# Self attention with its keys first, and cross attention's small steps at other places of its pipeline

## The chip, the cores and the metric

The kernel runs on 1 core of one Trainium2 chip, in one launch. The metric is the device time of one execution in microseconds (us); the time before is 2896.58 us, the median of 3 runs (2896.07 to 2899.03).

## The reference

Two Flamingo layers on x (16 x 56 x 256), each a gated attention block and a gated feed-forward block. What the change touches is the second layer's attention, which reads x and a context of 16 x 1500 x 256:

```python
ln_out = _ln(hidden_states, ln_w, ln_b)
q = _ln(_fp8_linear_pertensor(ln_out, wq, wq_scale, q_in_scale).reshape(b, s, g, hpg, d), qln_w, qln_b)
k = _ln(_fp8_linear_pertensor(ln_out, wk, wk_scale, k_in_scale).reshape(b, s, g, d), kln_w, kln_b)
v = _fp8_linear_pertensor(ln_out, wv, wv_scale, v_in_scale).reshape(b, s, g, d)
core = _gqa(q, k, v).reshape(b, s, nh * d)                 # self attention, 16 heads on 8 key groups
qx = _ln(_fp8_linear_pertensor(ln_out, wqx, ...), qxln_w, qxln_b)
kx, vx = jnp.split(jnp.einsum('bsi,oi->bso', cond, w_kv_x), 2, axis=-1)
xout = _gqa(qx, _ln(kx, kxln_w, kxln_b), vx)               # cross attention on 1500 context rows
cat = jnp.concatenate([core, xout], axis=-1)
catq = _div_clamp_fp8(cat, proj_smooth)                    # divide, clamp, round to fp8
```

`_fp8_linear_pertensor` scales its input per channel, clamps it and rounds it to fp8 before the product; `_gqa` is a softmax attention with two query heads for each key group.

## The kernel before

The program is a row of stages with a barrier of all engines between them. The change touches `self_attention` (L727) and `cross_attention` (L1217), and in `context_statistics` (L121) one index, by which the order of the scaled weight chunks is told.

**Self attention** goes over 8 pairs of batches (112 rows, a "turn"). A turn has 12 chunks of 4 heads (512 columns): 4 of the queries q, 4 of the cross attention's queries qx, 2 of the keys, 2 of the values. PE projects chunk t + 2 in slot t (L1016, high and low part of the weights). Each of the 10 normed chunks then runs through the engines: square on ACT (L900), sum of squares on DVE (L1127), root on ACT (L906), reciprocal and product on DVE (L1134, L1136), transposes on PE (L1027), scale and bias on ACT (L933). Tables of slots (L778 to L780) say where the rest lies: `SCORES` (PE L1037, L1040), `MAXIMA` (DVE L1142, L1146), `EXPS` (ACT L940), `SUMS` (DVE L1151, L1154 and POOL L865), `TURNED` (PE L1049), `VALUES` (ACT L946, PE L1060) and `OUTPUT` (DVE L1158 to L724, POOL L869, L874), each for four groups of heads of the turn before. `SCALED` and `QUANTISED` place the fp8 rounding of the inputs for the next two turns (ACT L953, DVE L1119 to L724, POOL L857, L861), one for each of q, qx, k and v: its parts go ACT, DVE, POOL, and the next one's scaling waits for them. Slots 12 and up of a table are slots of the turn after. Two turns make one pass of the loop; the body before lets the odd turn end with two roundings of inputs and two outputs. After the last turn, slots without chunks finish its attention.

**Cross attention** goes over 16 batches of 2 units (4 key groups, 448 query columns), 6 steps a unit, and each step treats 2 of the 12 context tiles of 125 rows. In step i, PE computes scores (L1468, 12 matmuls) and, 10 steps behind, the values (L1505, 12 matmuls); DVE takes the scores out of PSUM (L1556, s_sx), subtracts the maximum 8 steps behind (L1574), forms the low part of exp (L1580, s_p_lo) and the running maximum (L1593, s_mxh; in step 5 also L1598, s_mx); ACT does exp (L1422) and the high part (L1427); POOL adds the exps up (L1355, L1358, in step 1 also the last sum, L1361) and, in steps 1, 3 and 5 of a batch's second unit, splits the context (L1366, s_cn_lo). Around them lie the small steps, once a unit: step 0 transposes the maxima (PE L1514) and reduces them (DVE L1585); steps 1 and 2 fold the next unit's queries (PE L1445), which ACT and DVE split (L1383, L1541); step 2 spreads the maxima (L1475) and sums the exps of the unit two back (L1528), whose reciprocal (DVE L1569, step 3) ACT and PE spread (L1404, L1480, L1417, steps 3 and 4); step 5 multiplies by the value weights (PE L1489). One PSUM bank, `misc`, holds transposes, folds, sums, spread reciprocals and value products in turn. Step 0 of the next unit then multiplies products and reciprocals (DVE L1561, s_ca), rounds them (DVE L1602 to L1606; POOL L1370, L1374) and SP stores them (L1317). SP's queue is in order: it also loads the context in both layouts (L1299, L1300, L1305) and the queries (L1311), each load behind a wait for its buffer.

## Time and profile before

| | |
|---|---|
| median of 3 runs | 2896.58 us (2896.07 to 2899.03) |
| the profiled execution | 2896.9 us, its span 2895.1 us, mean granted clock 0.940 |
| PE, DVE, ACT, POOL busy | 88%, 74%, 38%, 32% of the span |
| self attention | 1033 to 1400 us of the span |
| cross attention | 1400 to 2660 us |

Busy shares are of the whole span; what a part costs is read from the stretch of its stage. The profile's own execution is 0.3 us above the median. The granted clock is given as a share of 2.4 GHz, so 0.5 is 1.2 GHz.

### The profile page before, as it was taken

The numbers are of one execution on the slowest core, as the hardware profiler recorded it, in microseconds if no ns is written. First come the engines' busy times: TensorE is split into PE (matmuls) and PEld (weight loads), VectorE is DVE, ScalarE is ACT, GpSimd is POOL, SyncE is SP. The second block draws the span as 40 slices with busy tenths as digits, with TensorE's granted clock in tenths as the row PEclk, the third lists the DMA queues.
The fourth block names the chain that finished last, engine by engine and source line by source line (L and its number), as shares of the span: only waits on it lengthen the run. The fifth ranks groups of instructions, "written<-read, shape, count | busy, mean of one in ns | idle before, by whom it ended". The sixth has DMA issues, their size and how long they took to land. (4 is left out here: it accounts for less than half of the span.)

```text
span 2895.1 us, 39559 instructions
## 1 busy us (share of the span) xinstructions
PE 2545.1 (88%) x13434; PEld 2221.3 (77%) x13434; DVE 2156.1 (74%) x3892; ACT 1100.6 (38%) x1787; POOL 928.2 (32%) x584
## 2 busy tenths in 40 slices
PE   7999999939999957777699999999999999986797
PEld 5777777738999945666588888888888888875797
DVE  8777777773333367777488889999999999993377
ACT  1000000014444445556144444545444444444332
POOL 6560000000000012443255555555555555553000
PEclk9999999969999958888799999999999999998899
DMA  6444333120111030101322122222222222213311
GB/s 240 182 172 158 137 143 135 55 73 30 59 44 44 0 115 26 39 39 39 118 73 70 62 73 73 73 73 71 70 66 68 69 69 65 65 38 86 103 50 40
DMA packets 116412, 231.89 MB, mean 80 GB/s; under 512 B 22176, under 2 KB 94704, under 8 KB 112240
## 3 DMA queue, kind: packets, MB, share of 16 engines
q1 hardware_dynamic: 112880, 218.35, 22.2%
q0 software_dynamic: 3456, 12.58, 1.1%
q8 instruction: 40, 0.66, 0.1%
q14 instruction: 36, 0.29, 0.0%
HBM read 158.95 MB, written 71.96 MB: 80 GB/s over the span
## 5 line engine op out<-in xcount | busy, mean ns | idle before, releaser
L1358 POOL TENSOR_TENSOR s_acc<-s_acc,s_sx 125x896 f32<-125x896 f32 x128 | 356.4, 2784 | 249.0 <-ACT s_sx L1422 248.9
L290 DVE BATCH_NORM_STATS2 s_st<-ps 125x6 f32<-125x128 f32 x1536 | 316.2, 286 | 114.2 <-PE ps L246 112.4
L1422 ACT ACTIVATE s_sx<-s_sx 125x896 f32<-125x896 f32 x192 | 184.0, 959 | 461.4 <-DVE s_sx L1574 461.3
L1505 PE MATMUL ps<-s_p_hi,s_cn_hi 125*128 125x448 f32 x768 | 297.7, 388 | 7.3 <-DVE s_p_lo L1580 6.9
L1468 PE MATMUL ps<-s_qc_hi,s_ct_hi 128*125 128x448 f32 x768 | 294.5, 383 | 1.3 <-issue 1.3
L1556 DVE TENSOR_TENSOR s_sx<-ps,keep_krs 125x896 f32<-125x896 f32 x192 | 208.7, 1087 | 106.8 <-PE ps L1468 103.2
L1468 PE MATMUL ps<-s_qc_lo,s_ct_hi 128*125 128x448 f32 x768 | 286.0, 372 | 0.0
L1468 PE MATMUL ps<-s_qc_hi,s_ct_lo 128*125 128x448 f32 x768 | 285.4, 372 | 0.0
L1505 PE MATMUL ps<-s_p_lo,s_cn_hi 125*128 125x448 f32 x768 | 283.1, 369 | 0.0
L1505 PE MATMUL ps<-s_p_hi,s_cn_lo 125*128 125x448 f32 x768 | 282.8, 368 | 0.0
L246 PE MATMUL ps<-s_wk_hi,s_hi 128*125 128x512 f32 x768 | 246.5, 402 | 40.3 <-DVE s_st L290 21.8
L1580 DVE TENSOR_TENSOR s_p_lo<-s_sx,s_p_hi 125x896 fp32r<-125x896 f32 x192 | 264.3, 1377 | 4.9 <-ACT s_p_hi L1427 4.9
L845 POOL MEMSET s_mask<- 112x112 f32 x1 | 0.2, 185 | 794.9 <-POOLq L432 794.9
L246 PE MATMUL ps<-s_wk_hi,s_lo 128*125 128x512 f32 x768 | 243.3, 398 | 0.0
L246 PE MATMUL ps<-s_wk_lo,s_hi 128*125 128x512 f32 x768 | 243.3, 398 | 0.0
L666 DVE TENSOR_TENSOR s_g_lo<-s_g,s_g_hi 128x898 fp32r<-128x898 f32 x64 | 70.1, 1096 | 214.4 <-ACT s_g_hi L495 214.4
L229 ACT ACTIVATE s_hi<-s_raw 128x3000 fp32r<-128x3000 f32 x16 | 43.4, 2714 | 470.4 <-PE ps L246 466.3
L1574 DVE TENSOR_TENSOR s_sx<-s_sx,ps 125x896 f32<-125x896 f32 x192 | 206.4, 1075 | 1.1
L246 PEld LDWEIGHTS ps<-s_wk_hi,s_hi 128*125 128x125 f32 x768 | 143.3, 188 | 82.1 <-DVE s_st L290 28.4
L1593 DVE TENSOR_TENSOR s_mxh<-s_mxh,s_sx 125x896 f32<-125x896 f32 x128 | 197.7, 1545 | 0.1
L1427 ACT ACTIVATE s_p_hi<-s_sx 125x896 fp32r<-125x896 f32 x192 | 183.1, 954 | 11.3 <-DVE s_p_lo L1580 4.3
L246 PEld LDWEIGHTS ps<-s_wk_lo,s_hi 128*125 128x125 f32 x768 | 144.9, 189 | 37.3
(303 smaller groups left out, 6054.9 us busy)
## 6 DMA issues: line engine op xcount, KB each, us to landing
s_raw<-in_ctxt SPq DMA_DIRECT2D x16, 1500.0 KB, 7.3
ct_hi<-s_hi SPq DMA_DIRECT2D x16, 1500.0 KB, 10.4
ct_lo<-s_lo SPq DMA_DIRECT2D x16, 1500.0 KB, 13.6
s_ct_hi<-ct_hi SPq DMA_DIRECT2D x48, 500.0 KB, 3.8
s_ct_lo<-ct_lo SPq DMA_DIRECT2D x48, 500.0 KB, 4.5
s_cn_raw<-in_ctx SPq DMA_DIRECT2D x48, 500.0 KB
s_w<-in_w SPq DMA_DIRECT2D x16, 1024.0 KB, 5.3
qx<-s_qxs SPq DMA_DIRECT2D x16, 448.0 KB, 2.8
```

Of the source, the lines that this page charges most:

```text
L246: mm = pe.matmul(kx[0:TT, t % NB, h, :], a[:, k, TT * t:TT * t + TT], w[:, k, 512 * h:512 * h + 512], start=(n == 0), stop=(n == 5))
L290: ins = dve.bn_stats(st[:, G * t + g, :], kx[0:TT, t % NB, g // 4, DH * (g % 4):DH * (g % 4) + DH])
L666: dve.tensor_tensor(g_lo[r][:, :], g32[r][:, :], g_hi[r][:, :].bitcast(F32), ALU.subtract).then_inc(s["g_lo_ready"], 1)
L1358: pool.tensor_tensor(a, a, p[:, PR * w.pt:PR * w.pt + PR, :], ALU.add).then_inc(s["acc_ready"], 1)
L1422: act.activation(p, p, ACT.Exp).then_inc(s["exp_ready"], 1)
L1427: act.activation(p_hi[w.pr][:, :, :], p, ACT.Copy).then_inc(s["hi_ready"], 1)
L1468: mm = pe.matmul(sc[st % 2][:, j, :], a[:, k, at:at + TT], x[w.h][:, k, :], start=(c == 0), stop=(c == 5))
L1505: mm = pe.matmul(pv[:, k, :], x[:, t, k * P:k * P + P], y[w.vr][:, j, :], start=(t == 0 and c == 0), stop=(t == NT - 1 and c == 2))
L1556: dve.tensor_tensor(by_group(sx[w.h][:, tiles, :]), by_group(sc[st % 2]), krs_b[:, tiles, HG * w.h:HG * w.h + HG].unsqueeze(3).to_broadcas ...
L1574: dve.tensor_tensor(p, p, mb.unsqueeze(1).to_broadcast([TT, PR, QH]), ALU.subtract).then_inc(s["sub_ready"], 1)
L1580: dve.tensor_tensor(p_lo[w.lr][:, :, :], p, p_hi[w.lr][:, :, :].bitcast(F32), ALU.subtract).then_inc(s["lo_ready"], 1)
L1593: dve.tensor_tensor(mxh[:, :, :], a, sx[w.h][:, tiles, :], ALU.max).then_inc(s["mxh_ready"], 1)
```

## The change

Self attention: the chunks come in the order keys, q, qx, values. The scores of a turn then lie in slots 7 to 10 of the same turn and their maxima in 8 to 11; exps, sums, turned probabilities and values in slots 0 to 7 of the next, the outputs in 5, 6, 7 and 12 of it. The inputs' roundings lie in slots 4 (v) of an even turn, and 4 (k), 10 (q) and 11 (qx) of an odd one; three of them, not four, come ahead of the first turn. The side work on the key weights moves from slots 8 and 9 to 4 and 5 of the first turn.

Cross attention: the sums' matmuls move on PE from the end of step 2 to step 3, behind its scores and ahead of its values; DVE's second split of the folded queries comes first in step 3; the product s_ca moves to step 5 of the unit before, ahead of the running maximum; the rounding on DVE and POOL moves to step 3; SP's stores go one place back, behind the load of the next batch's queries and first context chunk, the second one into the next batch.

```diff
+PART = [0] * NQ + [1] * NQ + [2] * NK + [3] * NK
+TURN_OF = [2, 0, 1, 3]
+ORDER = [c for part in TURN_OF for c in range(CHUNKS) if PART[c] == part]
+KIND = [TURN_OF.index(PART[c]) for c in ORDER]
...
-        SCORES, MAXIMA, EXPS = (0, 1, 2, 3), (1, 2, 3, 4), (5, 5, 5, 5)
-        SUMS, TURNED, VALUES, OUTPUT = (6, 7, 7, 8), (8, 9, 10, 11), (9, 10, 11, CHUNKS), (10, 11, CHUNKS, CHUNKS + 5)
-        SCALED, QUANTISED = ({}, {7: 0, 9: 1, 10: 2, 11: 3}), ({0: 3}, {8: 0, 10: 1, 11: 2})
+        SCORES, MAXIMA, EXPS = (7, 8, 9, 10), (8, 9, 10, 11), (CHUNKS,) * 4
+        SUMS, TURNED = [tuple(CHUNKS + t for t in ts) for ts in ((1, 2, 2, 3), (3, 4, 5, 6))]
+        VALUES, OUTPUT = [tuple(CHUNKS + t for t in ts) for ts in ((4, 5, 6, 7), (5, 6, 7, CHUNKS))]
+        SCALED, QUANTISED = ({3: 3}, {3: 0, 9: 1, 10: 2}), ({4: 3}, {4: 0, 10: 1, 11: 2})
...
-                for kind in range(4):
+                for kind in range(3):
                     round_input(0, kind)
...
                 def scores(q, a):
-                    if a == 0:
-                        pe.wait_ge(s["tr_read"], NORMED * q + NORMED)
+                    pe.wait_ge(s["tr_read"], NORMED * q + NK + a + 1)
...
@@ cross attention, SP @@
                     for c in range(NCH):
                         load_cn(b, c)
+                    if not first(b) and not (static(b) and b == 1):
+                        store(b - 2, 1)
                     if more:
                         load_q(b + 1)
+                        load_ct(b + 1, 0)
                     if not first(b):
                         store(b - 1, 0)
                     if more:
-                        load_ct(b + 1, 0)
                         load_ct(b + 1, 1)
-                    if not first(b):
-                        store(b - 1, 1)
-                    if more:
                         load_ct(b + 1, 2)
@@ POOL @@
-                    if w.i == 0 and w.three_back:
+                    if w.i == 3 and w.three_back:
@@ PE @@
+                    if w.i == 3 and w.two_back:
+                        pe.wait_ge(s["acc_ready"], NPR * (w.u - 1))
...
+                        for j in range(HG):
+                            mm = pe.matmul(sums[:, j:j + 1], acc[w.h][:, 0, PAIR * j:PAIR * j + PAIR], keep.ones[0:TT, 0:1], start=True, stop=True)
+                        mm.then_inc(s["sum_ready"], 1)
@@ DVE @@
+                    if w.i == 3 and w.next and w.new:
+                        qc_split(w.u + 1, 1 - w.h, 1)
                     if w.new:
                         dve.wait_ge(s["sc_ready"], w.n + 1)
...
+                    if w.i == NPR - 1 and w.two_back:
+                        dve.wait_ge(s["rb_read"], w.u - 1)
+                        dve.wait_ge(s["v_ready"], w.u - 1)
+                        dve.tensor_tensor(ca[:, :], misc[:, 0:QH], rsc[:, :], ALU.mult).then_inc(s["v_read"], 1)
...
+                    if w.i == 3 and w.three_back:
+                        dve.wait_ge(s["v_read"], w.u - 2)
+                        if not (static(b) and w.u < 4):
+                            dve.wait_ge(s["cat_ready"], w.u - 3)
+                        dve.tensor_scalar(cb[:, :], ca[:, :], FP8_MAX, -FP8_MAX, ALU.min, ALU.max).then_inc(s["cb_ready"], 1)
...
```

How the instructions stand on DVE at the end of an odd turn of self attention, before: the last input's rounding of slot 11, then slot 0 with the third output and another input (s_ca to s_cc is an output, s_xb to s_xc an input).

```order
L1158 TENSOR_TENSOR s_ca<-ps,keep_rsmooth 128x448 [waits s4_pv_ready]
L1163 TENSOR_SCALAR s_cb<-s_ca 128x448 [waits s4_cat_ready,s4_pv_read]
L723 TENSOR_SCALAR s_ce<-s_cb 128x448 [waits s4_dve_steps]
L724 TENSOR_SCALAR s_cc<-s_ce 128x448 [waits s4_dve_steps]
L1119 TENSOR_SCALAR s_xb<-s_xs 128x448 [waits s4_xs_ready,s4_xq_ready]
L723 TENSOR_SCALAR s_xe<-s_xb 128x448 [waits s4_dve_steps]
L724 TENSOR_SCALAR s_xc<-s_xe 128x448 [waits s4_dve_steps]
L1134 RECIPROCAL s_hrs<-s_hstd 112x4 [waits s4_tr_ready,s4_hstd_ready]
```

And there now:

```order
L1144 TENSOR_REDUCE s_mx<-ps 112x4 [waits s4_scores_ready]
L1148 TENSOR_TENSOR keep_x<-ps,s_mx 112x448 [waits s4_mx_ready,s4_prt_ready]
L1121 TENSOR_SCALAR s_xb<-s_xs 128x448 [waits s4_xs_ready,s4_xq_ready]
L726 TENSOR_SCALAR s_xe<-s_xb 128x448 [waits s4_dve_steps]
L727 TENSOR_SCALAR s_xc<-s_xe 128x448 [waits s4_dve_steps]
L1136 RECIPROCAL s_hrs<-s_hstd 112x4 [waits s4_tr_ready,s4_hstd_ready]
```

The input's rounding now stands behind a maximum, which needs PE's scores; the outputs stand elsewhere.

On DVE in cross attention, step 5 and step 0 of the next unit, before:

```order
L1580 TENSOR_TENSOR s_p_lo<-s_sx,s_p_hi 125x896 [waits s5_pv_ready,s5_hi_ready]
L1593 TENSOR_TENSOR s_mxh<-s_mxh,s_sx 125x896 [waits s5_mxh_ready]
L1598 TENSOR_TENSOR s_mx<-s_mxh 125x448 [waits s5_mt_ready,s5_mxh_ready]
L1556 TENSOR_TENSOR s_sx<-ps,keep_krs 125x896
L1561 TENSOR_TENSOR s_ca<-ps,s_rsc 128x448 [waits s5_v_ready,s5_rb_read]
L1574 TENSOR_TENSOR s_sx<-s_sx,ps 125x896 [waits s5_v_read]
L1580 TENSOR_TENSOR s_p_lo<-s_sx,s_p_hi 125x896 [waits s5_pv_ready,s5_hi_ready]
L1585 TENSOR_REDUCE s_m<-ps 112x4 [waits s5_diag_ready,s5_mt_ready]
L1602 TENSOR_SCALAR s_cb<-s_ca 128x448 [waits s5_cat_ready]
L1604 TENSOR_SCALAR s_ce<-s_cb 128x448 [waits s5_cb_ready]
L1606 TENSOR_SCALAR s_cc<-s_ce 128x448 [waits s5_ce_ready]
```

Now, the same two steps:

```order
L1578 TENSOR_TENSOR s_p_lo<-s_sx,s_p_hi 125x896 [waits s5_pv_ready,s5_hi_ready]
L1582 TENSOR_TENSOR s_ca<-ps,s_rsc 128x448 [waits s5_v_ready,s5_rb_read]
L1604 TENSOR_TENSOR s_mxh<-s_mxh,s_sx 125x896 [waits s5_mxh_ready]
L1609 TENSOR_TENSOR s_mx<-s_mxh 125x448 [waits s5_mt_ready,s5_mxh_ready]
L1559 TENSOR_TENSOR s_sx<-ps,keep_krs 125x896
L1572 TENSOR_TENSOR s_sx<-s_sx,ps 125x896
L1578 TENSOR_TENSOR s_p_lo<-s_sx,s_p_hi 125x896 [waits s5_pv_ready,s5_hi_ready]
L1587 TENSOR_REDUCE s_m<-ps 112x4 [waits s5_diag_ready,s5_mt_ready]
```

The product stands between low part and maximum, and the rounding has left step 0.

On PE, from the last value matmul of step 2 to the first scores of step 3, before:

```order
L1505 MATMUL ps<-s_p_hi,s_cn_lo 128x448
L1528 MATMUL ps<-keep_ones,s_acc 112x1 [waits s5_mt_read,s5_acc_ready,s5_qc_lo_ready]
L1528 MATMUL ps<-keep_ones,s_acc 112x1 x3
L1445 MATMUL ps<-s_q,keep_wk 128x112 x4
L1468 MATMUL ps<-s_qc_hi,s_ct_hi 125x448 [waits s5_sc_read]
```

And now, with the end of step 3's scores:

```order
L1514 MATMUL ps<-s_p_hi,s_cn_lo 128x448
L1447 MATMUL ps<-s_q,keep_wk 128x112 [waits s5_qc_lo_ready]
L1447 MATMUL ps<-s_q,keep_wk 128x112 x3
L1470 MATMUL ps<-s_qc_hi,s_ct_hi 125x448 [waits s5_sc_read]
...
L1485 MATMUL ps<-keep_ones,s_acc 112x1 [waits s5_qc_lo_ready]
L1485 MATMUL ps<-keep_ones,s_acc 112x1 x3
L1514 MATMUL ps<-s_p_hi,s_cn_hi 128x448 [waits s5_lo_ready]
```

The four sums stand 12 score matmuls later, and nothing stands between the values of step 2 and the fold.

## Rows read from the trace of the kernel before

**Rows 1.** Busy time by stretch: self attention, cross attention; us, then busy (x count) of PE, PEld, DVE, ACT, POOL, PEclk, DMA share, GB/s.

```profile
1033.00:1400.00 367.00, 262.12 (x1270) 202.90 (x1270) 273.62 (x588) 206.09 (x390) 130.38 (x128) 0.79 0.15 53
1400.00:2660.00 1260.00, 1159.02 (x6112) 1042.16 (x6112) 1107.46 (x1028) 589.55 (x1043) 662.54 (x304) 0.98 0.22 70
```

**Rows 2.** Busy time by stretch: turns 0 to 3 of self attention, and its end.

```profile
1050.80:1092.50 41.70, 31.54 (x93) 20.89 (x93) 35.01 (x55) 23.61 (x43) 6.21 (x6) 0.62 0.31 98
1092.50:1124.90 32.40, 24.90 (x138) 18.89 (x136) 22.59 (x49) 23.03 (x46) 5.76 (x6) 0.89 0.05 20
1124.90:1168.80 43.90, 34.05 (x159) 26.47 (x158) 34.09 (x71) 24.56 (x49) 18.16 (x18) 0.77 0.10 38
1168.80:1203.60 34.80, 27.62 (x159) 22.34 (x157) 27.83 (x65) 22.52 (x45) 14.03 (x14) 0.90 0.09 34
1360.80:1400.00 39.20, 17.58 (x93) 14.05 (x92) 18.76 (x48) 8.54 (x15) 20.03 (x20) 0.78 0.08 30
```

**Rows 3.** Timeline around the start of turn 2: start, us, engine, what, idle before.

```profile
1131.63 0.69 DVE L1127 TENSOR_REDUCE s_hss<-s_sq 112x4 f32<-112x512 f32 x1 [2.40 <-ACT s_sq L900]
...
1132.99 1.25 PE L1060 MATMUL ps<-s_pt,s_vn 112*128 112x224 f32 x4 [1.66 <-DVE s_ca L1158]
...
1136.27 0.85 ACT L953 ACTIVATE s_xs<-s_yt,s_rscale 128x224 bf16<-128x224 f32 x2 [4.67 <-DVE s_xc L724]
```

**Rows 4.** Timeline of the end of self attention.

```profile
1358.81 0.69 DVE L1136 TENSOR_TENSOR s_qn<-ps,s_hrs 112x512 f32<-112x512 f32 x1
...
1370.38 0.58 ACT L940 ACTIVATE keep_x<-keep_x 112x448 f32<-112x448 f32 x1 [5.24 <-DVE keep_x L1146]
...
1375.68 0.61 DVE L1151 TENSOR_REDUCE s_sums<-keep_x 112x4 f32<-112x448 f32 x1
...
1396.00 1.03 POOL L874 TENSOR_TENSOR s_cats<-s_cs,s_cc 128x448 bf16<-128x448 f32 x1
```

**Rows 5.** Waits of PE in cross attention: what waited for what, us in total, times, longest.

```profile
PE ps L1528 <- issue: 33.3, 26, 1.5
PE ps L1514 <- DVE s_ca L1561: 23.5, 15, 1.7
PE ps L1528 <- POOL s_acc L1361: 4.0, 3, 2.2
```

**Rows 6.** Busy time by stretch: one batch of cross attention, from sums to sums.

```profile
1897.89:1972.98 75.09, 70.97 (x383) 64.11 (x383) 69.04 (x65) 36.68 (x66) 41.48 (x20) 1.00 0.22 71
```

**Rows 7.** Timeline of cross attention at the sums of a batch's first unit.

```profile
1935.26 1.14 POOL L1361 TENSOR_TENSOR s_acc<-s_acc 125x448 f32<-125x448 f32 x1
...
1936.49 0.33 PE L1528 MATMUL ps<-keep_ones,s_acc 125*112 125x1 f32 x2 [1.42 <-issue]
...
1941.09 1.09 DVE L1556 TENSOR_TENSOR s_sx<-ps,keep_krs 125x896 f32<-125x896 f32 x1 [2.74 <-PE ps L1468]
```

**Rows 8.** Timeline of DVE, POOL and PE, steps 4 and 5 of the unit before that and step 0.

```profile
1909.25 2.41 POOL L1366 TENSOR_TENSOR s_cn_lo<-s_cn_raw,s_cn_hi 125x1024 fp32r<-125x1024 f32 x1
...
1909.38 3.23 DVE L1580 TENSOR_TENSOR s_p_lo<-s_sx,s_p_hi 125x896 fp32r<-125x896 f32 x1
...
1918.65 2.84 POOL L1358 TENSOR_TENSOR s_acc<-s_acc,s_sx 125x896 f32<-125x896 f32 x1 [4.09 <-ACT s_sx L1422]
...
1919.54 2.43 DVE L1598 TENSOR_TENSOR s_mx<-s_mxh 125x448 f32<-125x448 f32 x1
...
1923.56 0.64 PE L1514 MATMUL ps<-keep_ident,s_mx 125*112 125x125 f32 x4 [1.58 <-DVE s_ca L1561]
...
1925.81 2.69 POOL L1358 TENSOR_TENSOR s_acc<-s_acc,s_sx 125x896 f32<-125x896 f32 x1 [1.62 <-ACT s_sx L1422]
...
1926.55 2.08 DVE L1604 TENSOR_SCALAR s_ce<-s_cb 128x448 uint16<-128x448 uint16 x1
1928.67 0.28 DVE L1606 TENSOR_SCALAR s_cc<-s_ce 128x448 bf16<-128x448 bf16 x1
...
1929.02 1.03 POOL L1370 TENSOR_TENSOR s_cs<-s_cb,s_cc 128x448 f32<-128x448 bf16 x1 [0.53 <-DVE s_cc L1606]
```

**Rows 9.** Waits of SP's queue in cross attention.

```profile
SPq L1317 <- POOL s_cat L1374: 811.1, 32, 37.7
```

More of the change, by code:

```diff
@@ L194, in _ @@
                 for c in range(CHUNKS):
-                    j, kind = c % 2, KIND[c]
+                    j, kind = c % 2, PART[c]
                     if c >= 2:
@@ L714 @@
 NORMED = CHUNKS - NK
-LAST = [NQ - 1, 2 * NQ - 1, 2 * NQ + NK - 1, CHUNKS - 1]
-KIND = [0] * NQ + [1] * NQ + [2] * NK + [3] * NK
+PART = [0] * NQ + [1] * NQ + [2] * NK + [3] * NK
+TURN_OF = [2, 0, 1, 3]
+ORDER = [c for part in TURN_OF for c in range(CHUNKS) if PART[c] == part]
+KIND = [TURN_OF.index(PART[c]) for c in ORDER]
+LAST = [max(c for c in range(CHUNKS) if KIND[c] == kind) for kind in range(4)]
 RING = 3
@@ L785, in self_attention @@
         beyond = lambda p: isinstance(p, int) and p >= NP
-        slots = lambda p: range(max(OUTPUT) + 1 if beyond(p) else CHUNKS)
+        slots = lambda p: range(max(OUTPUT) - CHUNKS + 1 if beyond(p) else CHUNKS)
         def at_slot(table, t, p, act):
             for a in range(NQ):
-                if table[a] == t and not early(p, 1):
-                    act(p - 1, a)
-                elif table[a] == t + CHUNKS and not early(p, 2):
-                    act(p - 2, a)
+                back, left = divmod(table[a] - t, CHUNKS)
+                if left == 0 and back >= 0 and not early(p, back) and not beyond(p - back if isinstance(p, int) else p):
+                    act(p - back, a)
         def input_work(table, t, i, r, act):
-            if t in table[r] and not (isinstance(i, int) and (i >= COUPLES or i == 0 and r == 0 or i == COUPLES - 1 and r == 1)):
+            if t in table[r] and not (isinstance(i, int) and i + r >= COUPLES):
                 act(i + r, table[r][t])
@@ L959, in turn @@
                         live = not beyond(p)
[L960 removed]
+                        if live and t < NORMED and t != EXPS[0] - CHUNKS + 1:
                             std_of(p, t)
@@ L966, in turn @@
                             weight_hi(t + AHEAD)
-                        if early(p, 1) and t == 9:
+                        if early(p, 1) and t == 5:
                             act.wait_ge(s["wk_psum"], 1)
@@ L977, in turn @@
                         input_work(SCALED, t, i, par, scale_input)
-                        if live and t == EXPS[0]:
+                        if live and t == EXPS[0] - CHUNKS:
                             std_of(p, t + 1)
@@ L989, in _ @@
                 act.wait_ge(s["yt_ready"], K2)
-                for kind in range(4):
+                for kind in range(3):
                     scale_input(0, kind)
@@ L1193, in _ @@
                     weight_lo(c)
-                for kind in range(1, 4):
+                for kind in range(1, 3):
                     quantise(0, kind)
@@ L1521, in run @@
                         pe.wait_ge(s["qc_lo_ready"], K2 * w.u + K2 + 1)
-                    if w.i == 2 and w.two_back:
-                        pe.wait_ge(s["acc_ready"], NPR * (w.u - 1))
-                        if w.one_back:
-                            pe.wait_ge(s["mt_read"], w.u)
-                        for j in range(HG):
-                            mm = pe.matmul(sums[:, j:j + 1], acc[w.h][:, 0, PAIR * j:PAIR * j + PAIR], keep.ones[0:TT, 0:1], start=True, stop=True)
-                        mm.then_inc(s["sum_ready"], 1)
                     if w.i == 2 and w.new and w.next:
```

61 lines of the change are left out of this document (27 added, 34 removed).

## The prediction

> **What bounds the kernel now.** I read busy time by stretch first, then the waits of PE and DVE in the two stages that change, then the timeline where a wait recurs. The sum is made against the profiled execution, 2896.9 us, which stands 0.3 us above the median of 2896.58. A measurement of this kernel can tell about 0.2% (5.8 us) from no change.
>
> The two stages are bound differently. Self attention takes 367 us, in which no engine is full: DVE is busy for 273.6, PE for 262.1, at a mean granted clock of 0.79 [rows 1]. It is chains between engines that end last. Look at the turns [rows 2]: turn 2 takes 43.9 us and turn 3 takes 34.8, with the same 159 matmuls; turns 4 and 6 repeat the first at 43.8 each, turns 5 and 7 the second. The 9.1 us between them lie where an odd turn ends: there DVE has outputs and input roundings one behind the other, and each link waits: DVE 2.40 us for a square, PE 1.66 us for the output product that frees its bank, ACT 4.67 us for the rounding [rows 3]. After the last turn come 39.2 us with PE busy for 17.6 of them [rows 2].
>
> Cross attention is bound by PE: a batch takes 75.09 us, PE is busy for 70.97 and DVE for 69.04 [rows 6]. What PE loses there recurs with every unit: 33.3 + 4.0 us before the sums L1528, and 23.5 us before the transposes L1514, for DVE's product s_ca [rows 5]. The wait before the sums has no name in the view ("issue"), but the timeline gives one: POOL's last sum ends at 1936.40 and the sums' matmul starts at 1936.49 [rows 7]. Together 60.8 us; two sums of about 1.3 us (33.3 in 26) and one product of 1.58 [rows 8] make the 4.1 us that separate 70.97 from 75.09. DVE has little room: it waits for PE in step 3 (2.74 us, [rows 7]) but runs behind PE in steps 4 to 1.
>
> **Self attention, part by part.** Work is neither added nor removed; 8 turns of the same instructions stand in other slots.
>
> - The end of an odd turn. Outputs leave slots 10, 11 and 12 for 5, 6, 7 and 12, the input roundings for q and qx stay in 10 and 11, now beside maxima, the one for k goes to slot 4. The value chunks in those slots have no normalising, so there DVE has room for a maximum and a rounding. What is late next is the chain of the normed chunks, as in an odd turn today. I take turns 2, 4 and 6 at turn 3's length: 3 x 9.1 = 27.3 us gained. Bounds: nothing, if outputs bring the same 1.66 us waits to slots 5 to 7; and about 10 us more, if all seven later turns lose another 1.5 of the 7 us in which DVE idles in turn 3 (34.80 less 27.83, [rows 2]). Nearest is turn 3 itself, which has outputs and maxima apart from roundings for most of its slots.
> - Turn 0 takes in four scores and maxima: on DVE 8 instructions of some 0.6 us (a reduction of this size takes 0.61, [rows 4]), 5 us, and the v rounding; DVE is busy for 35.0 of 41.7 us there, so most shows: 4 us lost. Turn 1 takes over a full turn's attention and goes from 32.4 towards 34.8 [rows 2]: 2.4 lost.
> - The last turn's attention. Today the last normed product starts at 1358.81 and the first sum of exps at 1375.68, 16.9 us later, with ACT idle 5.24 us before its first exp; from there to the last output it is 21.4 us to 1397.03 [rows 4]. Scores and maxima of the first groups will be done by then; what is left ahead of the sums are two maxima and the exps under them, some 5 us. Gain 16.9 - 5.4 = 11.5; the 21.4 us stay.
> - One input rounding fewer ahead of the first turn: 1 us, since slot 4 has to take it.
>
> Sum: -27.3 + 4 + 2.4 - 11.5 - 1 = -33.4, call it 33; bounds 8 and 45.
>
> **Cross attention, part by part.**
>
> - The sums behind the scores of step 3. Twelve large matmuls lie in between; a batch has 288 of them in its 70.97 busy us [rows 6], so twelve take 2 to 3 us, more than the 1.42 us of the wait [rows 7]: it goes wholly. DVE's reciprocal waits for them now, behind its own 1.09 us for s_sx [rows 7]; the four small matmuls fit under it: 0. Behind the reciprocal on DVE stand the subtraction and so the exp; ACT's spread of it (step 3) and PE's (step 4) have a step's time.
> - The second split of the queries first in step 3. DVE idles there for 2.74 us [rows 7] and the split needs 0.6: 0. If DVE were behind, the order would not matter, as the work is the same.
> - s_ca to step 5. PE no longer waits in step 0. DVE's wait for the value products is covered by three operations of 1.09 us behind the same scores: 0.
> - Rounding to step 3. In step 0 the middle one, s_ce, takes 2.08 us where its twin s_cc takes 0.28: it stands still until POOL's addition, which began at 1925.81, ends at 1928.50 [rows 8]. DVE operations with SBUF inputs alone and POOL exclude each other here: s_p_lo, issued 0.13 us behind a split of POOL, takes 3.23. In step 3 exps come late on ACT (behind its spread of the reciprocal), so the rounding is through before POOL adds: 1.8 us of standing go.
> - POOL's rounding, 1.03 us twice [rows 8], then lies behind the addition of step 3 and, in a batch's second unit, behind a split of 2.41. This is where I choose to see a new wait. DVE's low part and maximum of step 4 alternate with split and rounding, and run 1 us later than today. In step 5 the product gives POOL's addition time to start ahead of the running maximum; the next split then starts ahead of s_mx. Today s_mx ends at 1921.97, before the product for which PE waits [rows 8]; it would end about 1 + 2.4 us later, near 1925.4, and PE's transposes wait for s_mx instead, starting 2.0 us later than today. Of that 0.8 us are the sums, which now lie ahead of this place and not behind, and 1.4 are given back where the sums waited (2.0 - 0.8 - 1.4 = -0.2): the stretch from step 3 of a second unit to step 3 of the next first unit gains 0.4 us or less. The other stretch has no splits in these places; it loses its wait of about 1.2 us (33.3 in 26, less the 1.42 of the longer kind).
> - Stores and loads on SP. SP waits 811.1 us for s_cat in 32 waits [rows 9]; the product is stored three steps later. The next batch's queries now stand behind a store that is ready a step or two later than they were free to load; they have five steps of 6 us until their fold. The first context chunk moves ahead of a store. 0.
>
> A batch gains 1.6 us, 16 batches 26 us; bounds 0 and 60.8.
>
> **Sum:** 2896.9 - 33 - 26 = 2838.
>
> **The rivals.**
>
> *No new wait at s_mx.* If POOL's split in step 5 comes after s_mx, or PE finds it in time, the 60.8 us all go. For it: PE's floor of 70.97 lies above DVE's 69.04, of which 2 x 1.8 us of standing go. Against: [rows 8] shows DVE standing still three times in two steps. With self attention's 33: 2803. Chance 0.25.
>
> *Self attention gets only its shorter end.* The stalls at the boundary follow the outputs to slots 5 to 7, and of the 33 us 12 - 4 remain, 8 to 12 us: with 26 in cross attention 2861. For it: PE waits for s_ca outside the boundary too. Against: no input rounding stands beside the outputs any more, except k's in slot 4. Chance 0.20.
>
> *The rounding meets POOL in step 3, in every unit.* If the exp ends before DVE reaches s_cb, POOL's addition (2.1 to 2.8 us) takes the port, s_cb and s_ce stand still, and its own rounding (1.03) stands before the maximum: 3.1 us a unit, 32 x 3.1 = 99 us, against 33 in self attention and 20 that the first units gain at the sums: 2896.9 + 46 = 2943, slower. It decides from 57 / 16 = 3.6 us a batch on. For it: s_ce does so today. Against: exp in step 3 stands behind two pieces of ACT work, and DVE's slack takes a part. The Trainium skill, "SBUF — State Buffer", section "Who interferes with whom", has the rule: GpSimd and a VectorE instruction with two SBUF inputs, or in a 2-port mode, take turns on one port pair, and whoever starts first holds it for the whole instruction. By that rule the rival hangs on which of the two starts first in step 3, and a product with one input in PSUM stays clear of it; the trace agrees, 3.23 us for s_p_lo behind a split. Chance 0.06.
>
> *Gains and losses cancel:* the boundary stays and the second units lose what the first gain. 0.03. Queries that come late behind a store would lead to the same place.
>
> **How the numbers follow.** The forecast has 0.46, the rivals 0.25, 0.20, 0.06 and 0.03. The forecast's own range is 2820 to 2855. To hold 8 in 10, the range goes from 2800 (takes in the first rival) to 2870 (takes in the second). Faster 0.91, same 0.03, slower 0.06.
>
> **What would show it.** In the profile after: turns of 34 to 36 us all along, and no rows of ACT waiting 4 us and more for an input's rounding; the end of self attention under 30 us; L1485, the sums, without idle time before it; in place of "L1514 <- s_ca" a wait of the transposes for s_mx, 2 to 3.4 us once a batch; s_ce at 0.28 us; a batch of 73.5 us. A batch of 71 would make the first rival right, even turns of 43 us the second, s_ce or s_cb above 1 us the third. The prediction is wrong if a batch takes over 75 us, or if PE waits for queries or context.

## The result and the profile after

The changed kernel takes **2826.69 us** (median of 4 runs, 2825.39 to 2827.53) against 2896.32 us for the kernel before (4 runs, 2889.68 to 2899.03): a ratio of 0.9762, 95% interval 0.9745 to 0.978. The forecast was 2838.0 us in a range of 2800 to 2870: the forecast was 11 us too high; the terms that were off are named in the section on the prediction. The profiled execution has a span of 2824.1 us against 2895.1.

Busy time by stretch of the changed kernel, first the cross attention, then turns 0 to 3 and the end of self attention, which answer to [rows 1, 2]. Columns: us, then busy (x count) of PE, PEld, DVE, ACT, POOL, PEclk, DMA share, GB/s.

```profile
1369.20:2591.50 1222.30, 1147.44 (x6112) 1031.04 (x6112) 1042.55 (x1028) 593.72 (x1045) 653.08 (x304) 0.98 0.22 73
1051.70:1089.90 38.20, 29.33 (x120) 20.78 (x120) 34.98 (x57) 25.45 (x46) 7.43 (x6) 0.81 0.27 84
1089.90:1124.60 34.70, 27.95 (x157) 22.33 (x157) 28.45 (x64) 21.79 (x44) 11.98 (x12) 0.90 0.07 28
1124.60:1161.40 36.80, 29.18 (x159) 22.76 (x158) 29.49 (x72) 23.75 (x49) 18.14 (x18) 0.86 0.10 38
1161.40:1196.60 35.20, 30.10 (x159) 23.74 (x158) 27.83 (x66) 22.26 (x46) 14.02 (x14) 0.81 0.11 40
1305.10:1369.20 64.10, 38.89 (x204) 30.75 (x202) 39.78 (x96) 28.75 (x54) 25.81 (x26) 0.79 0.13 51
```

The same of the kernel before: its cross attention, and everything behind the start of its last turn.

```profile
1400.10:2662.60 1262.50, 1159.07 (x6113) 1042.21 (x6113) 1107.93 (x1028) 592.05 (x1045) 662.54 (x304) 0.97 0.22 70
1325.90:1400.10 74.20, 45.41 (x250) 36.51 (x249) 45.85 (x110) 30.59 (x57) 31.97 (x32) 0.84 0.09 33
```

Cross attention gives 40.2 of the 71.0 us. The rest lies in self attention: the cross attention starts at 1369.2 and not at 1400.1. The even turns take 36.7 to 36.8 us where they took 43.8 to 43.9, turn 0 takes 38.2 where it took 41.7, and from the start of the last turn to the end it is 64.1 us, not 74.2 (behind that turn 28.9, not 39.2).

Waits of PE in the changed cross attention (what waited for what; us in total, times, longest), which answer to [rows 5], then a batch, then a stretch of 28 units:

```profile
PE ps L1523 <- DVE s_mx L1609: 26.7, 17, 2.7
PE ps L1485 <- DVE s_qc_lo L1542: 10.6, 27, 0.6
```

```profile
2035.27:2108.77 73.50, 71.10 (x382) 64.06 (x383) 64.88 (x64) 36.79 (x65) 40.56 (x19) 1.00 0.22 72
1453.10:2481.70 1028.60, 995.30 (x5351) 897.00 (x5350) 907.52 (x896) 515.20 (x911) 565.27 (x265) 1.00 0.22 72
```

Of the 37.3 us in which the sums waited for POOL's last sum, one wait of 3.3 us is left, and in their place stand 10.6 us in which the sums wait for VectorE's second split of the queries; the 23.5 us for s_ca are 26.7 us for s_mx. That wait stands where it was forecast, with POOL's split ahead of s_mx as forecast; what brings the split there is looked at under e4. Timeline of the changed kernel, from step 4 of a second unit to step 0 of the next, and a rounding in step 3; it answers to [rows 8]:

```profile
2009.60 1.71 POOL L1376 TENSOR_TENSOR s_cat<-s_cs,s_cc 128x448 bf16<-128x448 f32 x1
2011.27 5.06 POOL L1360 TENSOR_TENSOR s_acc<-s_acc,s_sx 125x896 f32<-125x896 f32 x2
2012.33 2.02 DVE L1578 TENSOR_TENSOR s_p_lo<-s_sx,s_p_hi 125x896 fp32r<-125x896 f32 x1
...
2014.81 2.48 DVE L1604 TENSOR_TENSOR s_mxh<-s_mxh,s_sx 125x896 f32<-125x896 f32 x1
2016.30 3.22 POOL L1368 TENSOR_TENSOR s_cn_lo<-s_cn_raw,s_cn_hi 125x1024 fp32r<-125x1024 f32 x1
2017.32 2.67 DVE L1609 TENSOR_TENSOR s_mx<-s_mxh 125x448 f32<-125x448 f32 x1
2020.13 0.64 PE L1523 MATMUL ps<-keep_ident,s_mx 125*112 125x125 f32 x4 [1.63 <-DVE s_mx L1609]
...
2038.80 0.28 DVE L1594 TENSOR_SCALAR s_ce<-s_cb 128x448 uint16<-128x448 uint16 x1
```

POOL's split now starts ahead of s_mx, and s_mx (0.62 us when it meets nobody) takes 2.67. The bit operation s_ce takes 0.28 us in all 32 units, as was forecast; its median was 2.08 before.

**The early batches.** Here is what the forecast had not seen. The stretch of 28 units of the kernel before, a slow batch in it, and PE's instructions where its clock fell:

```profile
1487.50:2546.40 1058.90, 1000.81 (x5349) 904.17 (x5349) 967.87 (x897) 513.42 (x911) 580.08 (x266) 0.99 0.22 69
1603.60:1681.80 78.20, 73.96 (x383) 66.69 (x382) 69.05 (x65) 36.68 (x66) 41.48 (x19) 0.96 0.21 68
```

```profile
1514.88 0.95 PE L1528 MATMUL ps<-keep_ones,s_acc 125*112 125x1 f32 x8 [1.08 <-DVE s_qc_lo L1541]
1515.69 1.85 PE L1445 MATMUL ps<-s_q,keep_wk 128*128 128x112 f32 x8
1517.22 0.71 PE L1468 MATMUL ps<-s_qc_hi,s_ct_hi 128*125 128x448 f32 x1
1517.73 0.57 PE L1468 MATMUL ps<-s_qc_lo,s_ct_hi 128*125 128x448 f32 x1
```

Fourteen batches of 75.09 us would be 1051.3 us; they took 1058.9. The other 7.6 us are five short stretches of half clock (1.2 GHz), all before 1682 us, behind a wait for the sums and the small matmuls that follow it: a score matmul takes 0.57 us in place of 0.37. The 78.2 us batch has two of them and a mean granted clock of 0.96; from 1681.8 us on the clock is 1.00. In the changed kernel it is 1.00 over the 28 units.

### The profile page after: what moved, and what is told of

Same layout as the page of the kernel before. It is cut to its first block and busy times, and to the rows that moved or that the text cites. A ratio compares the mean times of both kernels' runs of the same rounds, so it can differ in the third digit from the quotient of the medians.

```text
span 2824.1 us, 39559 instructions
## 1 busy us (share of the span) xinstructions
PE 2517.3 (89%) x13434; PEld 2198.9 (78%) x13434; DVE 2076.9 (74%) x3892; ACT 1098.5 (39%) x1787; POOL 919.2 (33%) x584
## 5 line engine op out<-in xcount | busy, mean ns | idle before, releaser
L1360 POOL TENSOR_TENSOR s_acc<-s_acc,s_sx 125x896 f32<-125x896 f32 x128 | 322.2, 2517 | 222.7 <-ACT s_sx L1424 220.1
L1604 DVE TENSOR_TENSOR s_mxh<-s_mxh,s_sx 125x896 f32<-125x896 f32 x128 | 215.0, 1680 | 0.1
```

The lines of the kernel that those rows point to most:

```text
L1360: pool.tensor_tensor(a, a, p[:, PR * w.pt:PR * w.pt + PR, :], ALU.add).then_inc(s["acc_ready"], 1)
L1604: dve.tensor_tensor(mxh[:, :, :], a, sx[w.h][:, tiles, :], ALU.max).then_inc(s["mxh_ready"], 1)
```

## The experiments

The texts under "expected" are those on record. Spans are of the profiled execution; "cross stretch" is the time from the start of the cross attention to the first matmul of the output projection: 1262.5 us before, 1222.3 after.

### The two halves apart

e1_self_only: the new `context_statistics` and `self_attention`, with the old `cross_attention`.

> The new self attention with the cross attention of before. Of the 71.0 us between the two profiled spans, 30.9 lie in the self attention's stretch and 40.2 in the cross attention's. If the two halves are independent, this run takes 2896.3 - 31 = 2865 us, its turns start at the same distances as with the whole change (38.2, 34.7, 36.8, 35.2, ...), and its cross attention is that of before: batches of 75.1 us, the first six of them 76.4 to 78.2 us with a stretch of half clock of 3.4 us in each. Rival: the slow first batches hang on how the self attention ends (what TensorE did before them), not on the cross attention's own order; then they are gone here too, the cross attention takes 14 us less than before, and the run takes about 2851 us.

e2_cross_only: the reverse.

> The self attention of before with the new cross attention. If the halves are independent: 2896.3 - 40 = 2856 us, batches of 73.5 us from the first on, no stretch of half clock in them. By the rival, in which the slow first batches come from the end of the self attention of before: they are here too, the first six batches take 2 to 3 us more each, and the run takes 2896.3 - 26 = 2870 us.

Measured: e1 2859.26 us (ratio 0.9872, 0.9855 to 0.9889), e2 2861.1 us (0.9877, 0.9861 to 0.9894). The cross stretches:

```profile
1367.40:2626.10 1258.70, 1156.27 (x6112) 1039.43 (x6112) 1108.00 (x1028) 592.41 (x1045) 662.65 (x304) 0.98 0.22 71
```

```profile
1401.00:2625.70 1224.70, 1149.46 (x6113) 1033.05 (x6113) 1042.91 (x1028) 593.82 (x1045) 652.92 (x304) 0.98 0.22 73
```

The spans are 36.6 and 37.9 us shorter than before, together 74.5 against 71.0: the halves nearly add up. The new cross attention is 37.8 us shorter behind the old self attention too. It has no half clock in its 28 steady units behind either self attention. The old order keeps such stretches behind the new self attention, but fewer: three in e1 where the kernel before has five, and one in e3 below, whose only edit is in self attention. So they need the old order of the cross attention, and how many there are hangs on what runs ahead: the rival falls as it was written, and has a part in their number.

### Self attention: the keys' place or the roundings' slots

e3_roundings_apart, in the kernel before:

```diff
-        SCALED, QUANTISED = ({}, {7: 0, 9: 1, 10: 2, 11: 3}), ({0: 3}, {8: 0, 10: 1, 11: 2})
+        SCALED, QUANTISED = ({2: 3}, {3: 0, 6: 1, 8: 2}), ({3: 3}, {4: 0, 7: 1, 9: 2})
```

> The kernel of before, whole, with one edit: the slots at which ScalarE scales and GpSimd rounds the inputs of the coming turns are spread out (fourth input at slots 2 and 3 of a turn, the first three of the next couple at 3 and 4, 6 and 7, 8 and 9), so that none stands beside the scores, the exponentials or the output's rounding. My theory of the long turn starts (43.9 us of each second turn, 7.6 us of them ahead of its second chunk) is that GpSimd's output roundings of the last pair queue behind its input roundings, and TensorE waits for a chain of both: then this edit alone brings the turns 2, 4 and 6 from 43.9 to about 37 us and the run to about 2896.3 - 20 = 2876 us. Rival: the long start is the chain of the scores themselves, which stand at the head of the turn with the queries' chunks ahead of the keys' (scores wait for the last chunk's transposes, the maxima for them, the exponentials for these), and the keys' place does it: then the time stays within 5 us of 2896.

e10_keys_first_old_slots, in the changed kernel (with four roundings ahead of turn 0, as before):

```diff
-        SCALED, QUANTISED = ({3: 3}, {3: 0, 9: 1, 10: 2}), ({4: 3}, {4: 0, 10: 1, 11: 2})
+        SCALED, QUANTISED = ({}, {7: 0, 9: 1, 10: 2, 11: 3}), ({0: 3}, {8: 0, 10: 1, 11: 2})
...
```

> The changed kernel with the slots of the input roundings of before (and four of them ahead of the first turn, as before): the fourth corner beside before (2895.1 us profiled, self attention's end at 1400.1), the roundings moved alone (2869.5 us, 1383.1) and both (2824.1 us, 1369.2). If the long starts of the turns 2, 4 and 6 are the roundings' slots in either order, these turns grow by several us each here too (as 43.9 against 35.3 to 35.8 did in the order of before), the self attention ends near 1369 + 20 = 1389 and the run takes about 2846 us. Rival: in the new order the output's roundings stand at other slots (5 to 8 of the next turn), away from the old slots of the input roundings too; then the keys' place cures the turns by itself, they stay within 1 us of 35.2 and the run within 5 us of 2827 us.

Measured: e3 2870.27 us (0.9907, 0.9891 to 0.9924), e10 2835.78 us (0.9789, 0.9773 to 0.9805). With before and after they are the four corners. Each has here its stretch from the start of turn 2 to that of turn 7, and from there to the end. Before (its end stands in the result's section):

```profile
1124.90:1325.90 201.00, 156.98 (x781) 123.67 (x781) 158.02 (x343) 118.37 (x233) 82.47 (x82) 0.81 0.09 36
```

e3, new slots alone:

```profile
1128.50:1308.40 179.90, 141.32 (x782) 113.41 (x781) 145.17 (x338) 115.61 (x229) 80.52 (x80) 0.88 0.10 37
1308.40:1383.10 74.70, 44.56 (x250) 35.98 (x248) 46.00 (x111) 30.66 (x57) 32.03 (x32) 0.83 0.10 38
```

e10, keys first alone, with its turn 0:

```profile
1128.20:1317.20 189.00, 148.40 (x780) 117.22 (x781) 146.91 (x343) 114.89 (x230) 82.30 (x82) 0.81 0.10 37
1317.20:1380.80 63.60, 39.42 (x204) 30.95 (x202) 39.75 (x95) 28.80 (x55) 25.78 (x26) 0.78 0.14 51
1052.10:1092.60 40.50, 29.09 (x120) 20.28 (x120) 35.03 (x57) 25.37 (x46) 6.21 (x6) 0.82 0.26 78
```

After, both:

```profile
1124.60:1305.10 180.50, 146.35 (x784) 114.89 (x782) 144.23 (x344) 115.84 (x233) 82.50 (x82) 0.85 0.10 39
```

In the turns, the slots alone give 21.1 us, the order alone 12.0, both 20.5: once the roundings stand apart from the outputs, the keys' place adds nothing there. What the order adds is the end, 74.2 to 63.6 or 64.1 us, which the slots don't touch. So the stall at the boundary is the meeting of outputs and input roundings. Moving the roundings parts them; the new order, in which the outputs stand elsewhere too, does so in part, and e10 at 2835.78 us lands between its two forecasts (2846, and 2827 with 5 us either way). The rival of e3 (no gain from the slots) falls. The waits of ACT for a rounding fit this, in the kernel before and then in the changed one:

```profile
ACT s_xs L953 <- DVE s_xc L724: 25.6, 8, 4.7
```

```profile
ACT s_xs L956 <- DVE s_xc L727: 4.7, 4, 3.5
```

e3 came out 6 us under its forecast: its untouched cross attention is 8.6 us shorter than before's, with one stretch of half clock in the 28 units in place of five. Its self attention alone gave 17 us (start of cross attention at 1383.1, before 1400.1).

### The moves inside cross attention

Three small pieces of work move: the sums (S), the product with the reciprocal (P) and the rounding (R). All eight combinations were run behind the new self attention: the changed kernel with the pieces not named put back. e1 above stands for the one without any; it also has the old order of the stores and of the queries' splits, so that prices against it carry these two as well.

e4_sums_at_old_place:

```diff
-                    if w.i == 3 and w.two_back:
-                        pe.wait_ge(s["acc_ready"], NPR * (w.u - 1))
...
                     if w.i == 2 and w.new and w.next:
                         pe.wait_ge(s["qc_lo_ready"], K2 * w.u + K2 + 1)
+                    if w.i == 2 and w.two_back:
+                        pe.wait_ge(s["acc_ready"], NPR * (w.u - 1))
...
                     if w.i == 2 and w.new and w.next:
                         fold_queries(w.u + 1, 1 - w.h, 1)
```

> The changed kernel with the sums over the probabilities back at the end of step 2, behind which the second half of the folded queries stands. The prediction gave the sums' move 1.2 us a batch, from the wait of before for GpSimd's last accumulation. In the changed kernel that accumulation ends at 2030.8, ahead of the end of step 2 (the sums run at 2035.3), since GpSimd's rounding has left step 0. Theory: with the rounding gone the sums could have stayed, 0 to 0.3 us a batch, the run takes 2827 to 2832 us. Rival: the place itself is worth the 1.2 us a batch: 2826.7 + 16 x 1.2 = 2846 us.

e5_product_at_old_place:

```diff
+                    if w.i == 0 and w.three_back:
+                        dve.wait_ge(s["rb_read"], w.u - 2)
+                        dve.wait_ge(s["v_ready"], w.u - 2)
+                        dve.tensor_tensor(ca[:, :], misc[:, 0:QH], rsc[:, :], ALU.mult).then_inc(s["v_read"], 1)
...
-                    if w.i == NPR - 1 and w.two_back:
...
```

> The changed kernel with the products with the reciprocal (s_ca, 0.6 us on VectorE) back at step 0 of the next unit, ahead of the folded queries' rounding, so that the transposes of the maxima wait no longer behind it and instead step 0 carries it. Theory: VectorE is the engine that ends last at a unit's start, and 0.6 us there is worth 0.6 us a unit or 1.2 us a batch: the run takes 2826.7 + 19 = 2846 us. Rival: VectorE waits 7.7 us a batch for TensorE's scores, six times, and one product is hidden in that wherever it stands: within 3 us of 2827 us, or, since it leaves the maxima's step, up to 10 us faster.

e6_rounding_at_old_place (VectorE's three instructions move likewise, behind the maximum):

```diff
-                    if w.i == 3 and w.three_back:
+                    if w.i == 0 and w.three_back:
                         d = w.u - 3
                         pool.wait_ge(s["cc_ready"], d + 1)
...
```

> The changed kernel with the rounding to 8 bits back at step 0 on VectorE (four operations) and on GpSimd (two, 1.9 and 1.7 us), sums and products at their new steps. Theory: GpSimd's accumulations of steps 1 to 3 come later by the 3.6 us of its two operations and VectorE's bit operation meets GpSimd again (2.08 us in place of 0.28), so this is what made the batch 75.1 us: each batch takes 1 to 1.6 us more than 73.5 and the run 2843 to 2852 us. Rival: the new places of the sums and the products have taken the waits out, and the rounding's place is free: within 4 us of 2827 us.

e11_rounding_alone (the edits of e4 and e5), e15_product_alone (e4 and e6), e16_sums_alone (e5 and e6):

> The changed kernel with the sums and the products with the reciprocal at their old steps: of the three moves in the cross attention the rounding's alone is left. The stretch from the cross attention's start to the output projection took 1222.3 us with all three moves, 1194.1 us without the sums' move, 1263.4 us without the products', 1292.1 us without the rounding's, and 1258.7 us in the run with the cross attention of before. If each move has its own price whatever the others do, sums +28, products -41 and rounding -70, this one takes 1194.1 + 41 = 1235 us and the run 2837 us. Rival: the three only shift VectorE against GpSimd, and which of the two then slows the other decides, so that no sum over the moves holds: the rounding alone could give anything from 1194 to 1292 us, and by that the price of the sums' move here (against 1263.4) is not 28.

> The changed kernel with sums and rounding at their old steps: the products' move alone. With a price for each move: 1292.1 - 28 = 1264 us for the stretch, the run 2866 us. Rival, in which the transposes of the maxima stop waiting for s_ca (23.5 us over 15 waits before) and nothing else changes: 1258.7 - 23 = 1236 us, the run 2837 us. By the third reading, in which the old place of the rounding on GpSimd (step 0) holds VectorE at the batch's start wherever the products stand: 1255 to 1262 us, no gain, 2855 to 2862 us.

> The changed kernel with products and rounding at their old steps: the sums' move alone, of which the prediction had counted 1.2 us a batch gained, from the wait for GpSimd's last accumulation. With a price for each move: 1258.7 + 28 = 1287 us for the stretch, the run 2888 us. By the prediction's term: 1258.7 - 19 = 1240 us, the run 2841 us.

Measured, with the cross stretch of each, the time that PE is busy in it (with the same matmuls in every run) and its mean granted clock:

| moved | run | us | ratio to before (95%) | cross stretch | PE busy | clock |
|---|---|---|---|---|---|---|
| none | e1 | 2859.26 | 0.9872 (0.9855 to 0.9889) | 1258.7 | 1156.27 | 0.98 |
| S | e16 | 2874.64 | 0.9924 (0.9907 to 0.994) | 1272.9 | 1175.34 | 0.96 |
| P | e15 | 2873.1 | 0.9914 (0.9897 to 0.993) | 1278.0 | 1170.67 | 0.97 |
| R | e11 | 2818.62 | 0.9727 (0.9711 to 0.9744) | 1218.7 | 1150.82 | 0.97 |
| S, P | e6 | 2892.23 | 0.9984 (0.9975 to 0.9994) | 1292.1 | 1186.29 | 0.95 |
| R, S | e5 | 2866.65 | 0.9894 (0.9878 to 0.9911) | 1263.4 | 1167.61 | 0.96 |
| R, P | e4 | 2797.42 | 0.9654 (0.9638 to 0.967) | 1194.1 | 1146.81 | 0.98 |
| R, P, S | after | 2826.69 | 0.9762 (0.9745 to 0.978) | 1222.3 | 1147.44 | 0.98 |

The rounding helps in every company (by 40.0, 9.5, 83.9 and 69.8 us); the product's move costs 19 us without the rounding's and gives 25 to 41 with it; **the sums' move costs in every company, 14 to 45 us**. No sum over prices holds, as the rival of e11 said. All three forecasts with fixed prices missed (1235 for 1218.7, 1264 for 1278.0, 1287 for 1272.9), and so did those of e4 to e6.

These prices are not all waits. PE has the same matmuls everywhere; where it is busy for longer they ran slower, and the mean granted clock is lower there. Without the rounding's move, the sums' move adds 19.1 and 15.6 us of busy time, more than its whole price of 14; beside the rounding it is 16.8 of 44.7. In e16 the sums of one unit wait 2.30 us for s_qc_lo, and the stretch behind them, 1865.0 to 1871.8 us, has a granted clock of 0.52. Beside both other moves, which is the step from e4 to the change, it is 0.6 of 28.2 us, and there the waits account for the price: 10.6 us for s_qc_lo, and 26.7 less 8.7 us for s_mx. Why some of these orders bring half clock all through the stage and others do not was not tested.

e4 beats both kernels: 29 us under the changed one. One batch of it, then its waits of PE for s_mx:

```profile
2016.14:2087.32 71.18, 70.75 (x383) 64.24 (x382) 63.39 (x65) 36.64 (x65) 42.84 (x19) 1.00 0.23 75
```

```profile
PE ps L1516 <- DVE s_mx L1609: 8.7, 16, 2.7
```

PE is busy for 70.75 of 71.18 us, and there is hardly anything left to take from its waits. The sums and the same place of the pipeline as above, of e4:

```profile
1996.95 1.05 POOL L1376 TENSOR_TENSOR s_cat<-s_cs,s_cc 128x448 bf16<-128x448 f32 x1
1997.83 1.12 DVE L1578 TENSOR_TENSOR s_p_lo<-s_sx,s_p_hi 125x896 fp32r<-125x896 f32 x1
1997.96 5.92 POOL L1360 TENSOR_TENSOR s_acc<-s_acc,s_sx 125x896 f32<-125x896 f32 x2
1999.40 2.50 DVE L1604 TENSOR_TENSOR s_mxh<-s_mxh,s_sx 125x896 f32<-125x896 f32 x1
2001.93 2.43 DVE L1609 TENSOR_TENSOR s_mx<-s_mxh 125x448 f32<-125x448 f32 x1
2003.84 2.78 POOL L1368 TENSOR_TENSOR s_cn_lo<-s_cn_raw,s_cn_hi 125x1024 fp32r<-125x1024 f32 x1
2004.49 0.64 PE L1516 MATMUL ps<-keep_ident,s_mx 125*112 125x125 f32 x4 [0.38 <-DVE s_mx L1609]
...
2016.14 0.85 PE L1529 MATMUL ps<-keep_ones,s_acc 125*112 125x1 f32 x8
```

Two things are to be seen. The sums have no idle time before them at their old place, since POOL's rounding has left step 0 and its last sum is done by then: the rounding's move had already removed the wait that the sums' move was meant to remove. e11, with the rounding's move alone, shows the same: of the waits for POOL's last sum one of 3.4 us is left. In step 3 the sums wait for s_qc_lo instead (10.6 us above, 36.9 us in e16), because they share the bank `misc` with the fold. And s_p_lo is first on its port by 0.13 us here (1997.83 against 1997.96) and takes 1.12 us; in the changed kernel POOL's addition is first by 1.06 us and s_p_lo takes 2.02. From then on s_mx is ahead of POOL's split here and behind it there. The Trainium skill, "SBUF — State Buffer", section "Who interferes with whom", says that whoever starts first holds the shared port pair for the whole instruction; both timelines agree, 1.12 against 2.02 us. Why the delay at the sums flips that meeting was not tested.

The forecast gave the split's place ahead of s_mx to the product's move. Without the rounding's move that holds in the batch looked at: the split starts ahead of s_mx in e15 and e6, behind it in e16. Beside the rounding's move it does not: the split is behind s_mx in e11 and e4, with the product in either place, and ahead of it in e5 (below) and the changed kernel. There it goes with the sums' move.

With the product at its old place beside the moved rounding and sums (e5), PE waits for s_ca as before, with the stall of s_mx now ahead of it:

```profile
2036.44 2.68 DVE L1610 TENSOR_TENSOR s_mx<-s_mxh 125x448 f32<-125x448 f32 x1
...
2040.04 0.61 DVE L1565 TENSOR_TENSOR s_ca<-ps,s_rsc 128x448 f32<-128x448 f32 x1
```

```profile
PE ps L1524 <- DVE s_ca L1565: 46.3, 15, 3.3
```

46.3 us against the 26.7 of the changed kernel. Of the 41.1 us by which this stage is longer, another 20.2 are busy time of PE. The transposes write the bank that s_ca reads, and s_ca stands behind s_mx and s_sx: it ends at 2040.65, 1.5 us behind s_mx, where I had counted its own 0.6.

### The split that stands ahead of s_mx

e7_third_split_later, in the changed kernel: at step 0 POOL does the third split of the batch before, at step 11 none.

```diff
                     c = cn_chunk(b, st)
+                    if st == 0 and not first(b):
+                        cb_, c = b - 1, NCH - 1
+                    elif c == NCH - 1:
+                        c = None
+                    else:
+                        cb_ = b
...
```

> The changed kernel with one edit: GpSimd's split of the third part of a batch's context stands at step 0 of the next batch in place of step 11. The prediction counted 1.6 us a batch of 75.1, because the transposes at the start of the next batch wait for the maxima, which share their step with that split (the maxima took 2.67 us in place of 0.6 there, and TensorE's last wait of a batch for them is 2.7 us with 26.7 us over all its places). If that is what holds the batch at 73.5 us, it falls to about 71.7 us here, and the run takes 2826.7 - 28 = 2799 us. Rival: GpSimd is the last by then in any case and the split only moves: the next batch's matmuls against the low part wait for it at its first use, by up to the 5.1 us that an addition on GpSimd takes and 3.2 us of its own; then the batch is 73.5 to 76 us and the run takes 2827 to 2865 us.

Measured: 2833.85 us (0.978, 0.9764 to 0.9797), 7 us slower than the change. The wait for s_mx is gone as forecast, and a new one has taken its place. Waits of PE in its cross attention:

```profile
PE ps L1453 <- DVE s_qc_lo L1548: 25.6, 18, 2.1
PE ps L1491 <- DVE s_qc_lo L1548: 16.8, 29, 0.6
...
PE ps L1529 <- DVE s_mx L1615: 3.9, 3, 2.6
```

```profile
2027.49 3.13 DVE L1584 TENSOR_TENSOR s_p_lo<-s_sx,s_p_hi 125x896 fp32r<-125x896 f32 x1
2030.54 3.01 DVE L1610 TENSOR_TENSOR s_mxh<-s_sx 125x896 f32<-125x896 f32 x1
```

In step 1 the split now stops s_p_lo, the addition behind it stops s_mxh, and the second fold waits for VectorE. My theory falls. The rival's time holds (2827 to 2865), but not by its reason, since PE waits for the low part only once, 1.1 us: the price of meeting the split moves with the split.

### The stores

e12_stores_at_old_place, in the changed kernel:

```diff
-                    if not first(b) and not (static(b) and b == 1):
-                        store(b - 2, 1)
                     if more:
                         load_q(b + 1)
-                        load_ct(b + 1, 0)
                     if not first(b):
                         store(b - 1, 0)
                     if more:
+                        load_ct(b + 1, 0)
                         load_ct(b + 1, 1)
+                    if not first(b):
+                        store(b - 1, 1)
+                    if more:
                         load_ct(b + 1, 2)
...
```

> The changed kernel with SyncE's stores of the outputs back at their old places among the loads. The prediction gave the move of the stores 0 us. If so: 2824 to 2830 us, batches of 73.5 us. Rival: the first batches of before (76.4 to 78.2 us, with a stretch of half clock each) were slow because a store stood ahead of a load of the next batch's context; then they are slow here too, and the run takes 2826.7 + 3 to 15 us.

Measured: 3088.61 us, ratio 1.0664 (1.0646 to 1.0681), 262 us above the change. Neither theory was near. Waits of PE and of SP's queue in its cross attention:

```profile
PE ps L1470 <- DMA s_ct_lo<-ct_lo: 227.9, 27, 13.1
```

```profile
SPq L1319 <- POOL s_cat L1376: 1151.8, 32, 51.2
```

The rounding in step 3 makes s_cat ready three steps later; SP's queue stands at the store (up to 51.2 us, in the changed kernel up to 37.6), and the load of the context behind it comes late. Of the 266 us by which the stage is longer 56 are busy time of PE (1203.85 us at a mean granted clock of 0.90) and 210 idle time. What the stores' move does beside the old place of the rounding was not run by itself; beside the new one, leaving it out costs 262 us.

## Why the prediction was right, and where its terms were off

By terms of the sum, all of them read from the profiled executions:

- **Even turns, -27.3 forecast, -21.3 measured** (43.9, 43.8 and 43.8 us to 36.8, 36.7 and 36.7). The cause was right, roundings beside outputs, and e3 and e10 show it. The size came from taking turn 3 as the nearest; an even turn still has 1.6 us more than an odd one. Turns 3 and 5, forecast as unchanged, take 0.8 us more together.
- **Turn 0, +4 forecast, -3.5 measured.** This step failed by its sign. The 8 instructions of maxima were put into the turn. By VectorE's groups of instructions in the changed turn 0, only three lie in it, and the rest in turn 1:

```profile
L1144 DVE TENSOR_REDUCE s_mx<-ps 112x4 f32<-112x448 f32 x2 | 1.2, 614 | 0.0
L1148 DVE TENSOR_TENSOR keep_x<-ps,s_mx 112x448 f32<-112x448 f32 x1 | 0.6, 625 | 0.0
```

VectorE is as busy as it was, 34.98 us in place of 35.01, in a shorter turn. PE's mean granted clock in it was 0.62 [rows 2] and is 0.81; whether that is the gain was not tested. With four roundings ahead and the old slots (e10) the turn takes 40.5 us; that run changes both, so the 2.3 us can't be given to one of them.
- **Turn 1, +2.4 forecast, +2.3 measured. The end, -11.5 forecast, -10.1 measured.**
- **One rounding fewer ahead of the first turn, -1 forecast, +1 measured.** The first projection starts at 1051.72 us where it started at 1050.76, behind a wait for POOL's s_xq of 7.51 us in both. PE's transposes ahead of it start 1 us later too, so dropping the rounding shortened nothing; where the 1 us comes from stays open.
- **A batch, -1.6 forecast, -1.59 measured** (75.09 to 73.50), with the waits in the places named: s_mx in place of s_ca, s_ce at 0.28 us. Sixteen batches make 25.4 us. Cross attention gave 40.2, and what is missing from the forecast is 7.6 us of half clock in the early batches, which I never looked for because I read one steady batch; the remaining 7 us lie at the two ends of the stage. These went from 87.4 to 83.9 and from 116.2 to 109.8 us, with PE busy for 6.1 us less and a granted clock of 0.91 and 0.89 where it was 0.88: by that the clock again, for the most part.
- **Right total, wrong attribution: in this part luck.** The prediction gave the gain of about 1.2 us at one of a batch's two sums to their new step, and at most 0.4 us to the half of the batch with the splits around s_mx. It came the other way round: from sums to sums that half went from 38.60 to 37.54 us, the other from 36.49 to 35.96. The eight runs show the sums' step to cost 28 us in this change; the rounding's move takes POOL out of step 0 and ends that wait by itself. The 1.6 us a batch came out because product and rounding together gave 3.9 (a batch of e4 takes 71.18 us) and the sums took 2.3 back.
- **The signs.** A batch of 73.5 us, s_ce at 0.28 us, an end under 30 us (28.9), s_mx waits of up to 2.7 us and no long wait of ACT for a rounding (3.5 at most) came as named. Turns of 34 to 36 us all along did not (turn 0 takes 38.2, the even ones 36.7 to 36.8), nor sums without idle time before them (10.6 us).
- **Stores: 0 forecast as a part of the whole, and so it is; 262 us if left out.** The prediction looked at what the new order delays, and not at what the old order would have cost once s_cat is late.
- **The rivals.** The first (2803 us, no new wait at s_mx) is nearly what e4 reaches, 2797.42. The second (self attention only its shorter end) is excluded by the turns. The third, a rounding that meets POOL in step 3, did not occur: s_ce takes 0.28 us in every unit. Two numbers of the working do not follow from its terms: the lower bound for self attention comes to 6 us and not 8, and the third rival's 33 and 20 us make 53 and not 57. Neither changes the forecast.

## What to carry to other kernels

When an edit moves several small steps, try each alone and each left out before keeping them all: here three moves gained 36 us together, one of them cost 28 of what the other two gave. Before work is moved away from a wait, ask whether another part of the edit already removes what it waits for. Look at the granted clock and the busy time beside the waits, and at the first batches beside a steady one: a move that adds small waits can cost more in clock than in waiting. And a store that shares a queue with loads has to move with the work that fills it.

## What the runs showed that was not expected

In one pair of timelines a lead of 0.13 us decides between VectorE and GpSimd who stands still: s_p_lo took 1.12 us when it was first, and 2.02 to 3.13 us behind POOL. The same instructions, in eight orders that differ by a step or three for small work, made cross stretches from 1194.1 to 1292.1 us, which is 6 us a batch; 39.5 of these 98 us are longer busy time of PE for the same matmuls, at a mean granted clock of 0.95 against 0.98. In the kernel before, the granted clock fell to half behind waits of 1.1 to 1.5 us that small matmuls followed, in the first batches and not in later ones, where a wait of 1.42 us [rows 7] is as long. What parts the early from the later batches stays open. So does why moves in self attention alone changed the number of these stretches from five to three and one.
